# Prepared keys and values for two attention layers: kv jobs by context group, value rows and fp16 keys laid out by GpSimd, rotary queries projected twice

## The reference, cut to what matters

```python
x = x + _L0_xattn_ref(_layernorm(x), ctx, ctx, ...)      # autocorrelation
x = x + _L0_ffn_ref(_layernorm(x), ...)                  # quantised feed-forward
x = x + _L1_xattn_ref(_layernorm(x), ctx, ctx, ...)      # windowed attention
x = x + _L1_ffn_ref(_layernorm(x), ...)                  # slots (soft mixture of experts)
x = x + _L2_xattn_ref(_layernorm(x), ctx, ctx, ...)      # full attention
x = x + _L2_ffn_ref(_layernorm(x), ...)                  # receptance
x = x + _L3_xattn_ref(_layernorm(x), ctx, ctx, ...)      # rotary attention
x = x + _L3_ffn_ref(_layernorm(x), ...)                  # routed experts

def _L3_xattn_ref(query, key, value, Wq, bq, Wk, bk, Wv, bv, Wo, bo):
    def proj(x, W, b):
        return (jnp.einsum('bsd,ed->bse', x, W) + b).reshape(B, S, H, Hd).transpose(0, 2, 1, 3)
    q, k, v = proj(query, Wq, bq), proj(key, Wk, bk), proj(value, Wv, bv)
    q = q * cos + rotate_half(q) * sin
    k = k * cos + rotate_half(k) * sin
    attn_w = jax.nn.softmax(jnp.einsum('bhqd,bhkd->bhqk', q, k) * scale, axis=-1)
    out = jnp.einsum('bhqk,bhkd->bhqd', attn_w, v)
    return jnp.einsum('bsd,ed->bse', out.transpose(0, 2, 1, 3).reshape(B, S, D), Wo) + bo
```

## Time and profile before

| | |
|---|---|
| median of three runs | 2014.44 us (2012.35 to 2026.28) |
| profiled execution, its time | 2015.01 us |
| its span, first to last instruction | 2013.3 us |
| quantised_ffn | 125 to 326 us |
| slot stage | 469.9 to 1373.75 us |
| full attention (at2) | 1373.75 to 1497 us |
| rotary attention (at3) | 1559.9 to 1695 us |

### The profile page before, as it was taken

One profiled execution on the slowest core, in us unless ns is written; L12 is line 12 of the kernel. 1 busy time (PEld: TensorE's weight loads), 2 busy tenths in 40 slices (PEclk: granted clock), 3 DMA queues, 4 the chain that ended last, 5 costly groups with the idle time before them and its releaser, 6 DMA issues. The chain is left out here.

```text
span 2013.3 us, 40727 instructions
## 1 busy us (share of the span) xinstructions
PE 1799.9 (89%) x15896; PEld 1320.4 (66%) x15896; DVE 1480.2 (74%) x3023; ACT 1156.9 (57%) x1954; POOL 371.2 (18%) x379
## 2 busy tenths in 40 slices
PE   7959878896689999999999999996989698699997
PEld 6944456575266666666666666663666277588886
DVE  6986877665877777777777777678765776688885
ACT  3535884665356666666666666553653565377774
POOL 0000400361450000000000000004100610166664
PEclk9969999998899999999999999998999799799999
DMA  6120321003220000000000000002000202678885
GB/s 223 48 84 1 131 100 54 2 3 137 95 92 27 22 22 22 22 22 22 22 22 22 22 1 1 1 1 100 3 23 0 104 3 71 208 226 252 246 255 117
DMA packets 95054, 142.32 MB, mean 71 GB/s; under 512 B 13264, under 2 KB 72080, under 8 KB 94704
## 3 DMA queue, kind: packets, MB, share of 16 engines
q1 hardware_dynamic: 83952, 119.08, 17.7%
q0 software_dynamic: 10912, 20.63, 4.1%
HBM read 114.24 MB, written 27.54 MB: 70 GB/s over the span
## 5 line engine op out<-in xcount | busy, mean ns | idle before, releaser
L2777 PE MATMUL sl_ps_eo<-sl_w,sl_hT 128*128 128x256 f16 x3072 | 354.9, 274 | 0.8 <-DVE sl_hT L3043 0.7
L2754 PE MATMUL sl_ps_h<-sl_slot_inT,sl_w 128*128 128x512 f16 x1536 | 339.2, 380 | 1.8 <-ACT sl_h L2897 1.8
L2777 PEld LDWEIGHTS sl_ps_eo<-sl_w,sl_hT 128*128 128x128 f16 x3072 | 299.3, 98 | 36.7 <-DVE sl_hT L3043 1.3
L2897 ACT ACTIVATE sl_h<-sl_ps_h,sl_b1T 128x512 f32<-128x512 f32 x256 | 175.8, 687 | 175.4 <-PE sl_ps_h L2754 166.0
L2754 PEld LDWEIGHTS sl_ps_h<-sl_slot_inT,sl_w 128*128 128x128 f16 x1536 | 150.0, 98 | 178.7 <-ACT sl_h L2897 4.4
L3043 DVE TENSOR_TENSOR sl_hT<-sl_h,sl_hT 128x512 f16<-128x512 f32 x256 | 181.1, 709 | 98.8 <-ACT sl_hT L2900 94.5
L1230 POOL MEMSET at_v<- 128x2048 f32 x6 | 10.7, 1814 | 898.0 <-POOLq L86 898.0
L1154 DVE TENSOR_REDUCE at_neg_max<-at_ps 128x8 bf16<-128x1024 f32 x96 | 113.0, 1219 | 57.7 <-PE at_ps L850 57.7
L2279 PE MATMUL mo_ps_h<-mo_xgT,mo_w 128*128 128x256 f16 x1104 | 125.8, 275 | 3.1 <-issue 1.8
L3057 DVE SCALAR_TENSOR_TENSOR sl_result<-sl_ps_eo,sl_b 128x256 f32<-128x256 f32 x128 | 54.3, 424 | 95.6 <-PE sl_ps_eo L2777 91.4
L1028 ACT ACTIVATE at_probT<-at_ps 128x1024 f32<-128x1024 f32 x96 | 97.8, 1022 | 46.3 <-PE at_ps L881 46.3
(11 more groups left out here) (458 smaller groups left out, 3762.7 us busy)
## 6 DMA issues: line engine op xcount, KB each, us to landing
mo_w_raw<-in_L_ffn_W SPq DMA_DIRECT2D x46, 1024.0 KB, 7.6
sl_w_in<-in_L_ffn_w SPq DMA_DIRECT2D x16, 1024.0 KB, 5.2
at_probT<-values SPq DMA_DIRECT2D x8, 512.0 KB, 10.0
mo_b<-in_L_ffn_b SPq DMA_DIRECT2D x23, 128.0 KB, 4.0
values<-qf_prodT SPq DMA_DIRECT2D x11, 256.0 KB, 2.2
ac_attention_w<-L_attention_w SPq DMA_DIRECT2D x3, 768.0 KB, 13.0
w_pairs<-ac_w_pair SPq DMA_DIRECT2D x3, 768.0 KB, 3.2
keys<-qf_prodT SPq DMA_DIRECT2D x9, 256.0 KB, 2.1
```

What stands on the lines that cost most here:

```text
L2754: last = pe.matmul(ps_h[:, j % 2], w1[:, e % 2, w, k, j * P:(j + 1) * P], slot_inT[:, q % 2, x, k].rearrange("p b s -> p (b s)"), start=(k ...
L2777: last = pe.matmul(ps_eo[:, b % 2, 0:D], hT[:, hp, j, b * P:(b + 1) * P], w2[:, e % 2, w, j], start=(j, a) == (0, 0), stop=(j, a) == (HJ - ...
L2897: act.activation(h[:, j % 2], ps_h[:, j % 2], ACT.Gelu, bias=b1T[:, q // G4, j:j + 1], scale=1.0 / W_SCALE).then_inc(h_ready, 1)
```

## The change

In quantised_ffn the jobs go by context group first and then by layer. The first group's context is taken from a tile that the kernel has had in SBUF since the stage's start (`early.ctx_pair`); the first layer's weights go to a ring (`xn`) that is free earlier, and their load is issued after the maxima of x. There are seven slots, four of them where `product_parts` doesn't write; ACT waits for the stores of the other three only.

In the slot stage the swap DMAs and all other work of POOL come after `row_split` and the fourth `result_ready`. Each rotation job also casts its keys to fp16 and stores them (`keys_half`); eight further jobs do that for layer 2's keys; and 32 jobs load 128x256 values, add bv into a row of 128x512 that holds the ones as well, and store it (`value_rows`).

In at2 and at3 SP loads the fp16 keys into KT_max and the value rows into v1 (256 KB and 1 MB for a quarter); POOL's memsets, casts of keys and value adds are gone, as is the load of bv, and POOL casts QT in both. The weights for queries come first, WO last. PE no longer waits for the constants ahead of its first projection; DVE makes only the query bias ahead of the normalised x and the rest after the first two groups. In at3, POOL copies the weights for the queries with the halves swapped (`wq_turned`); PE projects each job with both; DVE adds the bias and multiplies by the table in one instruction out of PSUM, twice, and adds.

```diff
@@ attention, SP
+            if prepared:
+                load_weight(WQ)
             for tile, name in consts:
                 sp.dma_start(tile[:], K[name]).then_inc(consts_in, 16)
...
             if prepared:
-                load_weight(WQ)
+                sp.dma_start(bo[:], W["bo"].unsqueeze(0).to_broadcast([P, D])).then_inc(consts_in, 16)
+                for g in range(G4):
+                    sp.dma_start(KT_max[:, :, 4 * g:4 * g + 4].rearrange("p c b l -> p c (b l)"),
+                                 env.keys_half[layer][:, C * g:C * g + C]).then_inc(kh_in, 16)
                 for g in range(G4):
                     sp.dma_start(KT[:, :, 4 * g:4 * g + 4].rearrange("p c b l -> p c (b l)"),
                                  (env.keys_roped if rotary else env.keys[layer])[:, C * g:C * g + C]).then_inc(k_in[g], 16)
+                    sp.dma_start(v1[:, 4 * g:4 * g + 4].rearrange("p b j r d -> p b (j r d)"),
+                                 env.value_rows[layer][:, 4 * g:4 * g + 4]).then_inc(v_in[g], 16)
...
-            if prepared:
-                for g in range(G4):
-                    sp.dma_start(v_plain[:, 4 * g:4 * g + 4], env.values[layer][:, 4 * g:4 * g + 4]).then_inc(v_in[g], 16)
@@ attention, PE
                 if rotary:
-                    enough(pe, plain_ready, job - 1)
+                    pe.wait_ge(wq_swapped, 2)
+                    enough(pe, rope_link, job - 1)
+                    for i, weight in enumerate((wT[:, WQ], wq_turned)):
+                        project(job, turned_bank(job, i), weight, xT[:, :, :, 4 * g:4 * g + 4], o)
...
-            pe.wait_ge(consts_in, CONSTS)
-            pe.wait_ge(made_consts, MADE)
+                pe.wait_ge(made_consts, MADE)
             for g in range(G4):
                 for o in range(C):
                     project_queries(g, o)
-                    if rotary and (g, o) != (0, 0):
-                        swap_halves(C * g + o - 1)
@@ attention, DVE
+                    dve.wait_ge(proj_made, 2 * job + i + 1)
+                    return dve.scalar_tensor_tensor(tile[:, job % 2].rearrange("p (b l) -> p b l", l=L),
+                                                    ps[:, turned_bank(job, i)].rearrange("p (b l) -> p b l", l=L), bq_scaled[:, i, o:o + 1],
+                                                    table[:].unsqueeze(1).to_broadcast(four), ALU.add, ALU.mult)
...
             if prepared:
+                prepare_bias()
                 for g in range(2):
                     x_group(g)
-                prepare()
+                prepare_rest()
...
-                if g == FIRST_MAXIMA:
+                if g == (G4 - 1 if prepared else FIRST_MAXIMA):
                     for pair in range(2):
                         maxima(0, pair)
@@ attention, POOL
+            if rotary:
...
+                for half in range(2):
+                    pool.tensor_copy(halves[1][:, half], halves[0][:, 1 - half]).then_inc(wq_swapped, 1)
+            if not prepared:
+                for half in range(2):
+                    pool.memset(v1[:, half * B // 2:(half + 1) * B // 2, :, :, DH:], 1.0).then_inc(ones_made, 1)
@@ quantised_ffn
-            i, r = divmod(j, 4 * G4)
-            g, k = divmod(r, 4)
+            g, r = divmod(j, 4 * len(PREPARED))
+            i, k = divmod(r, 4)
             return i, g, k
+
+        def kv_ctx(g):
+            return env.early.ctx_pair if g == 0 else kv_ctx_later[:, g]
...
-                pe.wait_ge(kv_ctx_in[g], 16)
+                if g == 0:
+                    pe.wait_ge(env.early.wk_in, env.early.key_weights_in(1))
+                else:
+                    pe.wait_ge(kv_ctx_in[g], 16)
...
-            for s in range(3):
+            for s in range(KV_KEPT, len(kv_slots)):
                 act.wait_ge(kv_stored[s], 16 * len(range(s, KV_JOBS, len(kv_slots))))
@@ slot stage, POOL
+            def keys_ready(nth, layer, job):
+                pool.tensor_copy(key_half, key_plain).then_inc(half_made, 1)
+                pool.wait_ge(half_made, nth + 1)
+                pool.dma_start(env.keys_half[layer][:, job], key_half).then_inc(turn_out, 16)
+                if layer == LAYERS:
+                    pool.dma_start(env.keys_roped[:, job], key_plain).then_inc(turn_out, 16)
+                pool.wait_ge(turn_out, 32 * (nth + 1) if layer == LAYERS else 32 * JOBS + 16 * (nth + 1 - JOBS))
+
+            pool.wait_ge(row_split, NT)
+            pool.wait_ge(result_ready, 4)
             for half in range(2):
                 pool.dma_start(swapped(env.keys_swapped, half), swapped(env.keys[LAYERS], 1 - half)).then_inc(swap_out, 16)
-            pool.wait_ge(row_split, NT)
...
-                pool.dma_start(env.keys_roped[:, job], key_plain).then_inc(turn_out, 16)
-                pool.wait_ge(turn_out, 16 * (job + 1))
+                keys_ready(job, LAYERS, job)
...
+                for n in range(B):
+                    nth = B * i + n
+                    pool.dma_start(value_plain, env.values[layer][:, n]).then_inc(value_in, 16)
+                    pool.wait_ge(value_in, 16 * (nth + 1))
+                    pool.tensor_tensor(value_row[:, :, :, 0:DH], value_plain.rearrange("p (j r d) -> p j r d", j=HR, r=R),
+                                       value_bias.rearrange("p (j r d) -> p j r d", j=HR, r=R), ALU.add).then_inc(value_made, 1)
+                    pool.wait_ge(value_made, nth + 1)
+                    pool.dma_start(env.value_rows[layer][:, n], key_swap).then_inc(value_out, 16)
+                    pool.wait_ge(value_out, 16 * (nth + 1))
```

174 lines of the change are left out of this document (91 added, 83 removed).

## The result

The changed kernel takes 1992.62 us, the median of four runs (1989.71 to 1997.47), against 2015.83 for the kernel before in the same session; the ratio is 0.988 [0.984, 0.992]. That is 23.2 us or 1.2% faster; forecast were 1995 us, 20 us less.

| stage | before | after | difference |
|---|---|---|---|
| what precedes quantised_ffn | 125.8 | 125.6 | -0.2 |
| quantised_ffn | 200.8 | 197.3 | -3.5 |
| windowed attention | 143.3 | 146.4 | +3.1 |
| slot stage | 903.9 | 902.8 | -1.1 |
| full attention (at2) | 123.5 | 115.4 | -8.1 |

The account below looks back on a forecast made before the run. PE bounds the slot steps, busy 713.07 of 713.07 us, so gains lie only where PE waits. Terms -4.4 - 5 - 4 - 1.4 + 7 - 7.5 - 5 = -20.3 from 2015.0 give 1995 us, range 1986 to 2007.

Parts of the forecast that it names:

- quantised_ffn: First kv job and chain of scales 2.2 us earlier, ACT's store wait of 2.19 us gone: -4.4 us.
- Slot stage, start: DVE's wait for the b_rows load shortens as the swap's 2 MB no longer go ahead of it: -5 us.
- Row maxima: Slot stage's row-maximum section: without POOL's bursts, DVE's casts aren't stretched and PE's 4.29 us gap goes: -4 us.
- The step from 566.55: Slot step in which PE idled 1.43 us with POOL at work; that idle time goes: -1.4 us.
- What comes back: POOL's 70 us of work moved among the steady slot steps costs PE time, rotations 4.5 and the rest 2.5: +7 us.
- at2: Full attention: memset stall and PE's wait for constants go, then PE waits for WO's load: -7.5 us.
- at3: Rotary attention: start some 6.6 us earlier, turned maxima 1 to 2 us less than that: -5 us.
- POOL at its full rate: Rival: in the slot steps each us of POOL costs PE 0.25, +17.5 for +7, giving 2005 us; chance 0.14.
- Slower than before: Rival: POOL and DVE instructions exclude each other in every phase of the steps, up to 2058 us; chance 0.07.
- break-even: Share of POOL's 70 us reaching PE in the slot steps from which the change would be slower: 0.39.
- POOL costs nothing: Rival: POOL's work in the slot steps costs PE nothing, giving 1988 us, or 1986; chance 0.17.

Follow-up runs that it names:

- e1: The changed kernel, unaltered, run once more: 1997.89 us, ratio 0.990 to the kernel before.
- e10: The changed kernel, unaltered, timed in one session on one chip with e9: 1992.08 us, ratio 0.988 to the kernel before.
- e5: e3 with the first context group loaded again, the swap ahead of its waits and PE waiting for the attentions' constants: 1995.25 us, one run.
- e6: e3 with five slots as before, POOL memsets heading at2 and at3, and rotations not waiting for result_ready: 1989.43 us, one run.
- e9: e3's kernel, unaltered, timed in one session on one chip with e10: 1985.54 us, ratio 0.985 to the kernel before.
- e2: The changed kernel with each rotation waiting for a result phase, all its work kept: 1986.35 us, ratio 0.985 to the kernel before.
- e4: The changed kernel without the rotation's products and sums, all loads, casts and stores kept: 1981.26 us, one run.
- e7: e3 with at3's queries projected once and half-swapped by fp32 matmul, and WO loaded ahead of keys and values: 1983.61 us, one run.
- e3: The changed kernel with each rotation's three 128x512 instructions cut into twelve of 128x128: 1980.38 us, one run.

## Why the prediction was right

The time, 1992.6, lies in the range and 2.4 us from the forecast; the sum of terms, -20.3, stands against -17.6 between the two profiles and -23.2 between the medians. That the time is so near is in part luck: in e1 and e10 the changed kernel was 17.7 and 24.7 us faster than the kernel before, and terms that came out larger and smaller than forecast cancelled. By its own steps:

- **quantised_ffn**, -4.4 forecast, -3.5 measured. The first job moved by 2.3 (2.2 forecast), ACT's eviction being next, and the chain of scales by 2.0. The store wait went as a row, 2.19, and was worth 1.3 to 1.8. That the job's wait was for the context itself was half right: e5 shows that its place in the queue was the cause.
- **Slot stage, start**, -5 forecast, -4.3 measured (first dispatch 27.3 to 23.0). In this stage e5 moves the swap alone and brings 4.0 back, or 1.2 to 1.6 against the runs of lower clock there.
- **Row maxima**, -4 forecast, -5.6 measured (69.4 to 63.8 from the first dispatch to the second). From the first of the row-maximum matmuls to the turning of the maxima it is 40.3 and 36.3 us, so the forecast's 4.0; PE's idle time there fell by 3.0. The other 1.7 lies behind: 24 matmuls of the first result phase took 4.45 us before and 2.78 after, at a clock of 0.60 and 1.00. With POOL at work there, e6 had 1.00 as well, so I don't put these 1.7 down to the change.
- **The step from 566.55**, -1.4 forecast, -1.9 measured. PE's 1.43 of idle time have gone, as forecast: its successor is busy for all of its 27.19, at the same clock of 0.94. The rest of the length is chance; in e9 this step is 25.52 at a clock of 1.00.
- **What comes back**, +7 forecast, +10.9 measured. This is the term that was mis-sized. The rule behind it was right: bursts in the hidden phase cost, bursts in the result phase don't (those at 582.38 and, in e2, all eight left PE without a gap). But "a rotation with its stores should take about 13 us, half a step, so every second one meets a hidden phase: 4 x 1.13" took the smallest gap for all. Each long step has one gap in the hidden phase (1.22, 2.22, 1.50, 1.20), and a rotation at the very end of the result phase holds the dispatch as well (1.13, and 0.78 just ahead of it): 8.0 in place of 4.5. In one step the clock fell to 0.94, which e1 and e10 don't repeat; with the larger gaps of those runs the steps cost 11.5 and 10.5 all the same. And the 2.5 us for casts and adds were nothing: the 32 adds, 25.0 us of POOL, left the steps at 25.46, as did the casts alone in e4. The two errors partly cancelled.
- **at2**, -7.5 forecast, -8.1 measured. The turned maxima gained 9.5, some 2 more than I had reckoned, and don't wait for WO as I had them do (e7). The loop over the sequences gave 1.4 back; I had not foreseen that, and its cause is open. That the two nearly cancel is luck. Of the 9.5, e5 gives 3.3 to 3.9 to the waits for constants and e6 2.6 to 3.2 to the memset (by the clock of the run compared with); the rest, 2.4 to 3.6, was not separated, DVE's casts of QT being the candidate. Both terms that I had named are there.
- **at3**, -5 forecast, -4.9 measured. The maxima gained 6.1, 1.2 was given back later. Of the doubled projection, a worry among the steps, no worth shows either way (e7).

Of the rivals, *POOL at its full rate* (+17.5) falls with e3, in which the same POOL time costs nothing. *Slower than before* had the right mechanism, exclusion, and the wrong reach: the DVE row waits, but PE does so only where it has nothing else queued. Of the forecast's 70 us of POOL work 10.9 reached PE, a share of 0.16, and the break-even was 0.39. *POOL costs nothing* is what e3 made true.

The Trainium skill's rule on this (page "SBUF — State Buffer", section "Who interferes with whom") says that whoever issues first has the shared port pair for the whole instruction and that the other blocks and isn't throttled; a DVE instruction contends when it has two SBUF inputs and GpSimd's reads SBUF, or when it runs in a two-port mode. The traces agree with the blocking: a cast of 0.42 us became 1.49 beside 128x512 and at most 0.82 beside 128x128, so a row's loss goes by the length of the other's instruction. In which mode DVE ran a cast, no trace shows.

## What to carry to other kernels

In a kernel like this one, work for an idle GpSimd is to be priced by the length of its single instruction and by who waits for VectorE at that moment, not by its sum: the same rotations cost 10.9 us in 128x512 and nothing in 128x128. When such work is moved, first look in which phase the engine that bounds the stage has work queued ahead of VectorE. A late load is to be traced to what was issued ahead of it: up to 4 us at the slot stage's start and most of the gain in the first kv job came from the order of issue. And before a difference of 1 or 2 us between single runs is put down to an edit, the granted clock of that stretch is to be compared.

## What was not expected of the hardware

- The hold ends with the single POOL instruction: cutting it into quarters took DVE's loss from 1.06 to at most 0.40 us a row, at equal POOL time.
- A gap of 2.22 us in PE was once followed by a granted clock of 0.57 over the next 4 us, and that cost nearly as much again (1.9 us) as the gap. Gaps of 2.16 and 2.25 at the same kind of place, in e1 and e10, were followed by 1.00.
- 2 MB moved from DRAM to DRAM held back a load of 32 KB on another queue: it landed 11.6 us after its issue with the swap ahead and 4.2 without, and DVE waited 8.9 and 1.8 us for it.
- Unaltered work differs with the granted clock from run to run: the first kv job's 12 matmuls took 2.75 us in e10 (clock 1.00 from 224 to 228), 4.02 after (0.73) and 4.44 in e5 (0.62 from 223.5 to 228).
